# Second attention of a transformer on one core: dense projections, 32x64 score tiles with the mask in them, a new instruction order

## The reference

```python
q = split_heads(l @ Wq.T + bq)          # 16 heads of 8 channels
k = split_heads(x @ Wk.T + bk)
v = split_heads(x @ Wv.T + bv)
scores = einsum('bhid,bhjd->bhij', q, k) * 8 ** -0.5
allowed = jj // 4 <= ii                 # jj key position, ii query position
scores = where(allowed, scores, -inf)
attn = softmax(scores)
out = einsum('bhij,bhjd->bhid', attn, v)
x = x + out @ Wo.T + bo
```

## Time and profile before

| what | us |
|---|---|
| median of 3 runs | 1991.72 (1990.61 to 1992.4) |
| the profiled execution | 1981.9 |
| its span, from first to last instruction | 1980.0 |
| TensorE matmuls busy, whole span | 1402.0 (71%) |
| VectorE busy | 1198.5 (61%) |
| ScalarE busy | 715.2 (36%) |
| GpSimd busy | 578.3 (29%) |
| mean granted clock of TensorE | 0.813 |
| first and last instruction of attention1_stage on VectorE | 447.4 and 662.2 |

### The profile page before, as it was taken

One profiled execution on the slowest core, in us unless ns is written; L12 is line 12 of the kernel. 1 busy time (PEld: TensorE's weight loads), 2 busy tenths in 40 slices (PEclk: granted clock), 3 DMA queues, 4 the chain that ended last, 5 costly groups with the idle time before them and its releaser, 6 DMA issues. The chain is left out here.

```text
span 1980.0 us, 43468 instructions
## 1 busy us (share of the span) xinstructions
PE 1402.0 (71%) x14268; PEld 1104.6 (56%) x14268; DVE 1198.5 (61%) x3390; ACT 715.2 (36%) x1769; POOL 578.3 (29%) x1087
## 2 busy tenths in 40 slices
PE   6999889848999610399939999740199656566564
PEld 3777545525777510299929999620177544454353
DVE  4888479978888650144416666550011179969896
ACT  2666456645666200122205444300033212232232
POOL 4555111112110217300066541117400187211221
PEclk9999967868999755699959999855599867677576
DMA  4222000000000001377711110001277411010001
GB/s 149 51 51 52 24 2 3 3 2 24 22 20 20 3 9 52 94 204 204 200 46 42 37 37 19 5 0 52 80 191 198 126 43 34 0 33 11 0 1 43
DMA packets 109054, 108.26 MB, mean 55 GB/s; under 512 B 12656, under 2 KB 88432, under 8 KB 108784
## 3 DMA queue, kind: packets, MB, share of 16 engines
q1 hardware_dynamic: 100720, 89.61, 16.6%
q0 software_dynamic: 8192, 16.79, 3.0%
HBM read 81.19 MB, written 25.17 MB: 54 GB/s over the span
## 5 line engine op out<-in xcount | busy, mean ns | idle before, releaser
L2220 DVE COPY e_xT<-e_pX 128x256 f32<-128x256 f32 x72 | 30.5, 424 | 318.9 <-PE e_pX L2281 318.9
L2281 PE MATMUL e_pX<-W,e_rows 128*128 128x128 f32 x144 | 28.9, 284 | 213.5 <-DMA e_rows<-slots_in 212.3
L2292 PE MATMUL e_H<-e_xT,e_w_up 128*128 128x256 f32 x736 | 175.3, 386 | 1.2 <-DMA e_w_up<-in_f_dram 1.2
L2292 PEld LDWEIGHTS e_H<-e_xT,e_w_up 128*128 128x128 f32 x736 | 137.3, 194 | 18.2 <-DVE e_xT L2220 1.6
L2281 PEld LDWEIGHTS e_pX<-W,e_rows 128*128 128x128 f32 x144 | 18.6, 147 | 216.1 <-DMA e_rows<-slots_in 215.7
L2302 PE MATMUL e_pY<-e_w_down,e_h 128*128 128x128 f32 x992 | 125.9, 279 | 15.1 <-ACT e_h L2269 13.8
L2302 PEld LDWEIGHTS e_pY<-e_w_down,e_h 128*128 128x128 f32 x992 | 120.8, 193 | 27.7 <-issue 19.5
L2141 POOL DMA_INDIRECT slots_in<-R,r_put x96 | 92.0, 958 | 57.1 <-issue 29.0
L428 DVE TENSOR_REDUCE a_mx<-a_S 128x8 f32<-128x1024 f32 x64 | 78.1, 1220 | 32.0 <-PE a_S L513 31.8
L473 ACT ACTIVATE a_PT<-a_ST 128x1024 f32<-128x1024 f32 x64 | 65.5, 1024 | 79.1 <-PE a_ST L540 79.1
L2258 ACT ACTIVATE e_silu<-e_H 128x256 f32<-128x256 f32 x120 | 46.0, 383 | 124.1 <-PE e_H L2292 124.1
(11 more groups left out here) (415 smaller groups left out, 4202.5 us busy)
## 6 DMA issues: line engine op xcount, KB each, us to landing
e_w_up<-in_f_dram SPq DMA_DIRECT2D x40, 384.0 KB, 3.6
e_w_down<-in_f_dram SPq DMA_DIRECT2D x32, 322.0 KB, 3.1
e_rows<-slots_in SPq DMA_DIRECT2D x72, 128.0 KB, 3.0
slots_out<-e_y SPq DMA_DIRECT2D x72, 128.0 KB, 3.5
e_w_up<-in_f_dram SPq DMA_DIRECT2D x32, 256.0 KB, 3.7
e_w_down<-in_f_dram SPq DMA_DIRECT2D x40, 192.0 KB, 3.2
slots_in<-Y SPq DMA_DIRECT2D x32, 160.0 KB, 2.5
a_cK<-in_ctxT_dram SPq DMA_DIRECT2D x64, 64.0 KB, 1.8
```

The source lines that it names most:

```text
L2292: i = nc.tensor.matmul(H[:, banks * p + b, CHUNK * c:CHUNK * (c + 1)], up[:, p, at:at + P], xT[:, p, :], start=True, stop=True)
```

## The change

All of it is in `attention1_stage` and its constants.
- q and k are made by one dense 128x128 matmul each in pA (project) and copied by two activations with their bias to `qT`, three buffers deep (take_q). VectorE makes `spread` from it with one multiply (mask4, four heads in 32 channels), in one instruction for both batches.
- A half of the scores is four matmuls with a 32x64 weight tile and 256 columns, as in the stage before it. The mask comes first in each of the four places by a bf16 matmul of the same tile shape: `rows` picks the query, `hide` holds the hidden keys of 16 queries.
- exps is one activation of 1024 columns for both halves. P is transposed into one PSUM bank, so transpose_p(1) waits for take_pt(0).
- product_v alternates between the two batches (`b` is the inner loop).
- The output bias is added to X by GpSimd (lag 3), and residual is one add.
- pX lies in pA's bank, pY in pVZ's, which now has three uses.
- Lags: softmax 7 to 6, spread 5 to 4. The order on every engine is new, and all lists are straight.

```diff
-        blk = sb("blk", [P, 2, 2, P])
-        spread = sb("spread", [P, 2, 2, GH, T])
-        Pr = sb("Pr", [P, 2, 2, GH * T])
+        qT = sb("q", [P, 3, 2, P])
+        spread = sb("spread", [P, 3, 2, HG, T])
+        Pr = sb("Pr", [P, 2, HEADS * T])
...
-        S = ps("S", [P, 2, 512])
-        PTp = ps("PTp", [P, 2, 512])
-        pXY, pA, pVZ, pO = [ps(n, [P, 512]) for n in ("pXY", "pA", "pVZ", "pO")]
-        pX, pY, pV, pZ = pXY[:, 0:128], pXY[:, 128:256], pVZ[:, 0:128], pVZ[:, 128:256]
+        S = ps("S", [P, 2, 2, 512])
+        PTp = ps("PTp", [P, 512])
+        pA, pVZ, pO = [ps(n, [P, 512]) for n in ("pA", "pVZ", "pO")]
+        pX, pY, pV, pZ = pA[:, 384:512], pVZ[:, 256:384], pVZ[:, 0:128], pVZ[:, 128:256]
...
+            def add_bias(u, p):
+                done(pool, ln.s_xn, u)
+                nc.gpsimd.tensor_tensor(X[:, u, :], X[:, u, :], w("a1_bo"), ALU.add).then_inc(s_bo, 1)
+
+            pipeline(pool, NT, [(1, lambda u, p: ln.pool_rstd(pool, u, p)), (3, add_bias)], straight=True)
...
             def take_spread(u, p):
-                done(dve, s_blk, u)
-                free(dve, s_S, u, per=2)
-                for g in range(2):
-                    src = pA[:, 384 + T * g:384 + T * g + T].unsqueeze(1).broadcast_to([P, GH, T])
-                    i = nc.vector.scalar_tensor_tensor(spread[:, p, g], src, w("a1_bk")[:, g:g + 1],
-                                                       mask, ALU.add, ALU.mult)
-                i.then_inc(s_spread, 1)
+                done(dve, s_q, u)
+                free(dve, s_S, u, bufs=3, per=2)
+                src = qT[:, u % 3, 1].rearrange("p (b t) -> p b t", b=2).unsqueeze(2).broadcast_to([P, 2, HG, T])
+                nc.vector.tensor_tensor(spread[:, u % 3], src, mask, ALU.mult).then_inc(s_spread, 1)
...
-            pipeline(dve, NT, [(0, lambda u, p: ln.vector_stats(dve, u, p)),
-                               (1, lambda u, p: ln.vector_moments(dve, u, p)), (10, normalise),
-                               (2, lambda u, p: ln.vector_apply(dve, u, p)), (7, softmax(0)),
-                               (11, residual), (7, softmax(1)), (5, take_spread)])
+            pipeline(dve, NT, [(10, normalise), (2, lambda u, p: ln.vector_apply(dve, u, p)), (6, softmax(0)),
+                               (4, take_spread), (1, lambda u, p: ln.vector_moments(dve, u, p)),
+                               (0, lambda u, p: ln.vector_stats(dve, u, p)), (6, softmax(1)), (11, residual)], straight=True)
...
+            def take_q(u, p):
                 done(act, s_proj, u)
+                free(act, s_S, u, bufs=3, per=2)
+                free(act, s_spread, u, bufs=3)
+                nc.scalar.activation(qT[:, u % 3, 0, :], pA[:, 0:128], ACT.Identity, bias=w("a1_bq"))
+                nc.scalar.activation(qT[:, u % 3, 1, :], pA[:, 128:256], ACT.Identity, bias=w("a1_bk")
+                                     ).then_inc(s_q, 1)
+
+            def exps(u, p):
+                done(act, s_sub, u, per=2)
+                nc.scalar.activation(Pr[:, p, :], Pr[:, p, :], ACT.Exp, scale=SCALE).then_inc(s_exp, 1)
...
-            pipeline(act, NT, [(10, take_zt), (8, take_v), (3, take_xt), (8, take_pt(0)),
-                               (8, take_pt(1)), (7, exps(0)), (7, exps(1)), (4, take_blk)])
-
-
-        turnsXY = Bank(NT, {"y": (11, s_x, 1, 1), "xt": (3, s_xts, 1, 1)})
-        turnsVZ = Bank(NT, {"z": (10, s_zts, 1, 1), "v": (8, s_vs, 1, 1)})
+            pipeline(act, NT, [(8, take_pt(0)), (4, take_q), (7, exps), (8, take_pt(1)), (10, take_zt),
+                               (8, take_v), (3, take_xt)], straight=True)
+
+        turnsVZ = Bank(NT, {"z": (10, s_zts, 1, 1), "v": (8, s_vs, 1, 1), "y": (11, s_x, 1, 1)})
...
+                nc.tensor.matmul(pA[:, 0:128], w("a1_wq"), xT[:, p, :], start=True, stop=True)
+                nc.tensor.matmul(pA[:, 128:256], w("a1_wk"), cK[:, p, :], start=True, stop=True
+                                 ).then_inc(s_proj, 1)
...
+                    for b in range(2):
+                        for r in range(2):
+                            at = 64 * r + 32 * half
+                            nc.tensor.matmul(S[64 * b:64 * b + 64, half, r, 0:256], rows[at:at + 32, :],
+                                             hide[at:at + 32].rearrange("p h k -> p (h k)"),
+                                             start=True, stop=False)
+                    for b in range(2):
+                        for r in range(2):
+                            at = 64 * r + 32 * half
+                            i = nc.tensor.matmul(S[64 * b:64 * b + 64, half, r, 0:256],
+                                                 qT[at:at + 32, u % 3, 0, T * b:T * b + T],
+                                                 spread[at:at + 32, u % 3, b].rearrange("p h t -> p (h t)"),
+                                                 start=False, stop=True)
+                    i.then_inc(s_S, 1)
...
-                    for b in range(2):
-                        r = slice(64 * b, 64 * b + 64)
-                        for j in range(4 * g, 4 * g + 4):
+                    for j in range(4 * g, 4 * g + 4):
+                        for b in range(2):
+                            r = slice(64 * b, 64 * b + 64)
...
-            pipeline(pe, NT, [(10, transpose_z), (11, output), (9, product_v(0)), (9, product_v(1)),
-                              (8, values), (8, transpose_p(0)), (8, transpose_p(1)), (3, transpose_x),
-                              (6, scores(0)), (6, scores(1)), (4, project)])
+            pipeline(pe, NT, [(10, transpose_z), (8, transpose_p(0)), (6, scores(0)), (4, project),
+                              (8, transpose_p(1)), (8, values), (6, scores(1)), (11, output),
+                              (9, product_v(0)), (9, product_v(1)), (3, transpose_x)], straight=True)
```

More of the change, by code:

```diff
@@ L827, in attention1_stage @@
     SCALE = 8 ** -0.5
+    HG = 4
     with ExitStack() as ctx:
@@ L852, in attention1_stage @@
         s_xt, s_xts, s_proj = sem("xt"), sem("xt_out"), sem("proj")
-        s_blk, s_spread = sem("blk"), sem("spread")
+        s_q, s_spread = sem("q"), sem("spread")
         s_S, s_mx, s_sub, s_exp = sem("scores"), sem("max"), sem("sub"), sem("exp")
@@ L869, in load_for @@
                 return fn
-            pipeline(sp, NT, [(2, load_for(cK, s_cK, s_proj)), (4, load_for(cV, s_cV, s_v))])
+            pipeline(sp, NT, [(2, load_for(cK, s_cK, s_proj)), (4, load_for(cV, s_cV, s_v))], straight=True)
         @block.gpsimd
@@ L886, in _ @@
-            nc.vector.tensor_copy(allow[:, :], w("allow1")).then_inc(s_tb, 1)
-            nc.vector.tensor_copy(identb[:, :], w("ident")).then_inc(s_tb, 1)
+            mask = w("mask4").unsqueeze(1).unsqueeze(3).broadcast_to([P, 2, HG, T])
+            nc.vector.tensor_copy(hide[:, :, :], w("hide1").unsqueeze(1).broadcast_to([P, HG, T])
+                                  ).then_inc(s_tb, 1)
+            nc.vector.tensor_copy(rows[:, :], w("rows1")).then_inc(s_tb, 1)
             def take_spread(u, p):
-                done(dve, s_blk, u)
-                free(dve, s_S, u, per=2)
-                for g in range(2):
-                    src = pA[:, 384 + T * g:384 + T * g + T].unsqueeze(1).broadcast_to([P, GH, T])
-                    i = nc.vector.scalar_tensor_tensor(spread[:, p, g], src, w("a1_bk")[:, g:g + 1],
-                                                       mask, ALU.add, ALU.mult)
-                i.then_inc(s_spread, 1)
@@ new lines, in take_spread, with softmax @@
+                nc.vector.tensor_tensor(spread[:, u % 3], src, mask, ALU.mult).then_inc(s_spread, 1)
+            def softmax(half):
+                def fn(u, p):
+                    Sg = S[:, half, :, 0:256].rearrange("p r (h k) -> p r h k", k=T)
+                    top = mx[:, p].rearrange("p (r u h) -> p r u h", r=2, u=2)[:, :, half]
+                    out = Pr[:, p].rearrange("p (r u h k) -> p r u h k", r=2, u=2, k=T)[:, :, half]
+                    dve.wait_ge(s_S, 2 * u + half + 1)
+                    nc.vector.tensor_reduce(top, Sg, AX, ALU.max).then_inc(s_mx, 1)
+                    dve.wait_ge(s_mx, 2 * u + half + 1)
@@ L992, in transpose_x @@
                 done(pe, ln.s_xn, u)
-                turnsXY.take(pe, "xt", u)
+                free(pe, s_xts, u, bufs=1)
+                free(pe, s_q, u, bufs=1)
                 nc.tensor.transpose(pX, xn[:, p, :], w("ident")).then_inc(s_xt, 1)
@@ L998, in project @@
                 landed(pe, s_cK, u, p)
[L999 to L1007, removed]
@@ L1008, in project, with scores @@
-                i.then_inc(s_proj, 1)
-            def scores(g):
+                free(pe, s_q, u, bufs=1)
+                nc.tensor.matmul(pA[:, 0:128], w("a1_wq"), xT[:, p, :], start=True, stop=True)
+                nc.tensor.matmul(pA[:, 128:256], w("a1_wk"), cK[:, p, :], start=True, stop=True
+                                 ).then_inc(s_proj, 1)
+            def scores(half):
```

(19 more changed lines are left out.)

51 lines of the change are left out of this document (12 added, 39 removed), and 2 rows, old and new, of the table PACK.

## The result

The changed kernel takes 2140.18 us (4 runs, 2137.63 to 2152.49); the kernel before 1991.16 (4 runs, 1979.26 to 1992.4). The ratio is 1.0799 (1.0764 to 1.0834), about 159 us slower on a median of 1991; the two medians alone differ by 149 us, the two profiled executions by 155.7 (1981.9 and 2137.63). The forecast said 117 slower. By the ratio the time is 2151 us (2144 to 2158), 8 above the upper end of the range. The sign and the mechanism were right, the size was too small.

A forecast was written before the change was run, and what follows sets the result against it. TensorE set the pace at 6.32 us a tile; new waits make it 10.45: 26 x (10.45 - 6.32) = 107, +10 draining, on 1981.9 gives 2099, plus 9.8 to the median: 2109 us, range 2044 to 2143.

The forecast's parts named there:

- The loop: Second attention: values waits for take_zt, transpose_z for normalise; 8.0 us a tile at full clock, 11.5 at half, against 6.32.
- The rival in which the loop with VectorE decides: Second attention: bank wait does nothing, VectorE's loop sets 6.1 us a tile; 1986 us, chance 0.05.
- the rival by the sums: Second attention: buffers let engines run apart, TensorE's 5.24 us sets the tile; 1964 us, chance 0.08.
- I take a mean clock of 0.65: Second attention: TensorE's clock 3 parts in 10 full, giving 10.45 us a tile; mixed clock, 2065 to 2143, chance 0.60.
- filling: Ten first iterations of the stage: low clock but no wait, left as they were, plus or minus 5 us.
- draining: Seven last iterations: exps and take_pt(1) still stand ahead of take_zt for three, +10 us.
- the clock stays low throughout: Second attention at the low clock: 26 x 5.2 + 16 = 151 us more, 2143 us; no chance of its own.
- the bias add: Output bias add of 0.29 us moved from VectorE to GpSimd: nothing, or 0.3 to 0.6 us a tile if residual waited.
- straight code: Second attention's loop code becomes straight code: instruction fetch given nothing.
- a half of the scores: Each scores half on TensorE: slot of 0.74 us at full clock, 0.59 plus 0.15 for the mask.
- product_v at 1.20 with its switch: product_v on TensorE: 1.05 + 0.15 us against 1.25, pairing mostly there already through overlap; bounds 0.9 and 1.1.
- a switch of 0.15: TensorE: each change of the array's tile shape costs about 0.15 us; switches rise from four to seven a tile.

The follow-up runs named there:

- e4: Changed kernel in its own order, plus four extra unneeded fp32 matmuls ahead of values in each tile: 2080.50 us, ratio 1.0466 to the kernel before.
- e1: Changed kernel with only ScalarE's order different, take_zt and take_v moved ahead of exps and take_pt(1): 2073.03 us, ratio 1.0450 to the kernel before.
- e2: Changed kernel with only TensorE's order different, transpose_z after scores(0) instead of first: 2123.59 us, ratio 1.0663 to the kernel before.
- e3: Changed kernel with both new orders, ScalarE's of e1 and TensorE's of e2: 1974.30 us, ratio 0.9932 to the kernel before.
- e9: Changed kernel with take_zt moved to second place on ScalarE, take_v left behind exps and take_pt(1): one run, 2090.48 us, beside 1988.63 for the kernel before.
- e8: Changed kernel with thirty extra matmuls ahead of values in tile 4 only: one run, 2142.18 us.
- e5: Changed kernel with six extra matmuls ahead of values in each tile, instead of e4's four: 2092.88 us, ratio 1.0536 to the kernel before.
- e7: e3 with the bias add back on VectorE, two adds in residual: ratio 0.9933 to the kernel before.
- e10: Kernel before, with only its second attention written out straight instead of in a loop: ratio 0.9964 to the kernel before.
- e6: e3 with product_v unpaired, the loop over b outside as before: ratio 0.9981 to the kernel before.

## Why the prediction was right about the loop and wrong about the size

**The loop: right.** Values waits for take_zt behind take_q, exps and take_pt(1), and transpose_z waits for zn. At the full clock I had 8.0 us, e4 shows 8.04; at the half clock 11.5, the changed kernel shows 11.28. e1, e2, e3 and e9 take the links apart by the order alone: 6.1 against 6.23 at the full clock and 9.4 against 9.62 at the half one (e1), 10.5 against 10.64 at the half (e2), 5.24 against 5.28 (e3, in part by luck), 6.9 to 7.1 against 7.15 at the full and 10.0 to 10.6 against 9.78 at the half (e9). The rival in which the loop with VectorE decides (6.1) is what is left once ScalarE's order is changed (e1); the rival by the sums needs e3's orders. In the change's own neither held.

**The step that failed: "I take a mean clock of 0.65".** The clock was 0.50 in the whole stage. Instead of 10.45 us a tile 26 iterations took (777.3 - 484.6) / 26 = 11.26 on average; against 6.30 before that is 129 us where the sum had 107. The rest of the shortfall is at the ends: filling took 33.0 us to the first transpose_z instead of 29.2 (+3.8; I had 0, plus or minus 5), draining 45.1 instead of 21.6 (+23.5; I had +10, and +16 for the low clock). At both ends too the clock was 0.50, where the kernel before had 1.00 from 463 us on. 129 + 3.8 + 23.5 = 156.3, what the stage grew. The rival "the clock stays low throughout" had 2143 and was the case that came; its 151 us are near the 156 because its tiles were 6 us too dear and its ends 11 too cheap. I gave it the end of a range instead of a weight of its own.

Why 0.65 was wrong: I read the clock off the busy share of other stretches. That share is no measure of it. The changed kernel was busy 84% at 0.50, the stage before 87% at 0.80, e1 between 640 and 678 us 98% at 0.50, e3 96% at 1.00. At the half clock the same work takes nearly twice as long (product_v's loads 1.79 us for 1.01), so a high share is also what a low clock produces. The Trainium skill, "TensorE: Matmul & The Clock Gate", Why this matters for your kernels, warns of idle gaps longer than those here. This trace, with gaps of 1.97 and 0.57 us in each tile and the clock at 0.50 throughout, shows a low clock without such a long one, and e8 shows the raised clock falling right behind a gap of 2.22 us. In e1, where the loads in the tiles shown never stood idle for more than 0.90 us, it was mostly 0.50 too. That the waits do it and not the new shapes is shown by e3: the same matmuls in another order, no gap between loads above 0.64 us in the tile shown, clock 1.00. What exactly decides the level is not settled: e4 and e5 filled the long gap and still fell back in every second to fourth tile.

**Prices.** Right: project (0.50 in e3 with the switch, 0.44 forecast), the bias add at nothing (e7), straight code at no loss (e10). Too high: a half of the scores, 0.66 for 0.74, of it the mask 0.07 for 0.15. Wrong: product_v at 1.20 with its switch is 1.05 in e3 and 1.35 in e6. I had taken a switch of 0.15 out of its old slot of 1.25, although values follows it there in the same shape and no switch falls into that slot. Without it the old price is 1.25 / 32 = 0.039 a record and not 0.034, and the pairing was worth something after all: the 32 loads take 1.32 us in the earlier trace rows and 1.01 in e3.

## What to carry to other kernels

When engines' lists are reordered, follow each wait into the list of the engine that has to answer: what stands ahead of the answer in the same iteration is part of the tile. Sharing a PSUM bank between results of different lags makes such a link even where no data flow. Forecast each clock level as a case of its own and give the low one real weight as soon as TensorE waits in every tile; here the same loop cost 8.0 or 11.3 us, and one late wait a tile went with a clock of 0.50 throughout (e2, 1.97 us) or of 0.56 on average (e1, 0.57 to 0.90 us at transpose_z). With the new shapes a tile took 5.28 us for 6.31, and the order of the lists alone made 11.28 of it; the old shapes in e3's orders were not run. Count the filling and draining iterations as well: in e3 they took back half of what the tiles had gained.

## What the runs showed of the hardware

- Adding four matmuls to each tile made the kernel 60 us faster, and TensorE's mean clock rose from 0.50 to about 0.9 (e4).
- After a burst that stretched its tile from 11.3 to 22.7 us and lifted the clock to 1.00, the clock fell back to 0.50 within the next tile (e8).
- Matmuls whose weights fill half the columns went faster in alternating halves than eight records at a time in each: 32 records in 1.11 us instead of 1.42, with moving operands of only 18 columns (e3, e6).
- A busy share does not tell the clock: TensorE was busy 98% at 0.50 (e1, 640 to 678 us) and 96% at 1.00 (e3).
